# Score levels of a gated linear attention: from one head at a time to both heads in one pass, and a loop over sequences written out

## The reference, cut to what matters

```python
q = silu(x @ wq); k = sigmoid(x @ wk); v = x @ wv; f = 1 - k
g = log(f)                       # decay of each channel at each token
theta = cumsum(sign(f - 0.5)) * pi
qr = [q*cos, q*sin]; kr = [k*cos, k*sin]
# per token: S = S * exp(g) + k v^T ;  o = q S        (2 heads of 128 channels)
out = layernorm(out * sigmoid(x @ wg1 @ wg2)) @ wo
x = x + out                      # then layernorm, route to 1 of 8 experts, add
```

## Time and profile before

| | us |
|---|---|
| median of 3 runs | 716.99 |
| lowest and highest | 715.19, 717.59 |
| the profiled execution | 711.37 |
| its span, first to last instruction | 709.5 |
| routing begins | 378.98 |
| the experts' matmuls begin | 412 |

### The profile page before, as it was taken

How to read it: one execution, slowest core, us unless ns; L and a number is a source line. 1 busy time by engine, 2 the same in 40 slices (tenths; PEclk the granted TensorE clock), 3 DMA queues, 4 the chain that set the end, 5 groups by cost and what they waited for, 6 DMA issues and landing times. The chain is left out here.

```text
span 709.5 us, 13168 instructions
## 1 busy us (share of the span) xinstructions
PE 608.2 (86%) x3634; PEld 508.1 (72%) x3635; DVE 391.0 (55%) x951; ACT 281.4 (40%) x679; POOL 230.5 (32%) x344
## 2 busy tenths in 40 slices
PE   4789989869898999987463279999999999999993
PEld 2557667656666776776442179999999999999992
DVE  1486988848899898978626513323232333323231
ACT  4554667446574747654331022222222222222220
POOL 6414260511605234150302302333323233333321
PEclk9999999988999999998855579999999999999998
DMA  8900004140040302011023284554646465555410
GB/s 318 382 0 1 2 30 90 31 90 0 30 89 30 90 30 61 2 60 31 30 59 119 103 311 165 201 207 168 226 167 225 174 215 191 197 204 177 166 32 0
DMA packets 26842, 83.43 MB, mean 118 GB/s; under 512 B 3437, under 2 KB 13039, under 8 KB 20656
## 3 DMA queue, kind: packets, MB, share of 16 engines
q1 hardware_dynamic: 21120, 67.98, 28.9%
q0 software_dynamic: 4992, 14.45, 5.4%
q10 hardware_dynamic: 688, 0.52, 0.2%
HBM read 70.33 MB, written 13.52 MB: 118 GB/s over the span
## 5 line engine op out<-in xcount | busy, mean ns | idle before, releaser
L1447 DVE TENSOR_TENSOR arena<-bank_a,b_col 128x512 f32<-128x512 f32 x78 | 54.0, 692 | 190.7 <-PE bank_a L1109 177.0
L1109 PEld LDWEIGHTS bank_a<-masks,arena 128*128 128x128 f32 x1248 | 146.8, 194 | 1.9
L1109 PE MATMUL bank_a<-masks,arena 128*128 128x128 f32 x1248 | 146.9, 277 | 0.0
L1123 PE MATMUL bank_c<-w_sb,arena 128*128 x624 | 141.5, 380 | 0.9 <-ACT arena L844 0.9
L1123 PEld LDWEIGHTS bank_c<-w_sb,arena 128*128 128x128 f32 x624 | 115.5, 190 | 15.9 <-issue 1.8
L1178 DVE TENSOR_TENSOR arena<-arena 128x256 f32<-128x256 f32 x224 | 92.9, 457 | 22.1 <-PE bank_l L869 14.3
L869 PEld LDWEIGHTS bank_l<-arena,k_mix 128*128 128x128 f32 x448 | 67.1, 200 | 52.6 <-ACT k_mix L663 26.5
L869 PE MATMUL bank_l<-arena,k_mix 128*128 128x128 f32 x448 | 73.6, 290 | 18.8 <-ACT k_mix L663 11.9
L844 ACT ACTIVATE arena<-arena 128x512 f32<-128x512 f32 x78 | 45.0, 622 | 106.8 <-PE bank_c L1123 102.5
L834 ACT ACTIVATE masks<-bank_b,b_col,g_col 128x128 f32<-128x128 f32 x78 | 31.5, 453 | 132.7 <-PE bank_b L1097 132.7
L881 PE MATMUL bank_a<-arena 128*128 128x512 f32 x160 | 82.8, 616 | 0.0
(11 more groups left out here) (135 smaller groups left out, 811.0 us busy)
## 6 DMA issues: line engine op xcount, KB each, us to landing
arena<-w SPq DMA_DIRECT2D x39, 1024.0 KB
routed_rows<-arena SPq DMA_DIRECT2D x8, 1026.0 KB, 7.4
arena<-x SPq DMA_DIRECT2D x16, 512.0 KB, 3.8
w_sb<-w SPq DMA_DIRECT2D x8, 1024.0 KB, 14.2
arena<-b SPq DMA_DIRECT2D x1, 1024.0 KB, 4.3
arena<-routed_rows,take_now POOLq DMA_INDIRECT x39
out<-k_mix,put_now POOLq DMA_INDIRECT x39, 2.4
arena<-wk SPq DMA_DIRECT2D x1, 256.0 KB, 4.0
```

What stands on the lines that cost most here:

```text
L1109: m = pe.matmul(bank_a[k // 4][:, k % 4 * P:(k % 4 + 1) * P], w1_now[t.par][:, i * F + k * P:i * F + (k + 1) * P], xl_t[t.par % 2][:, i * ...
L1123: m = pe.matmul(bank_c[p][:, 0:D], h_act[:, k * P:(k + 1) * P], w2_sb[:, bass.ds(e * (FC * D) + k * D, D)], start=(k == 0), stop=(k == FC ...
L1447: dve.tensor_tensor(h_sb[:, n * 512:(n + 1) * 512].rearrange("p (k t) -> p k t", t=P), bank_a[n][:, :].rearrange("p (k t) -> p k t", t=P), ...
```

## The change

Every level function loses its head: one product loop over four pairs, one wait, updates of 512 columns, key copies of 256 columns. `need` counts semaphores per level and no longer per level and head. The pipeline loop is written out on every engine. The order on each engine is new as well: what stood between the two heads of a level now stands before or after the whole level.

```diff
@@ pipeline
-            for i in range(2):
-                at(i)
-            with eng.Fori(1, NSEQ // 2 - 1) as half:
-                for par in range(2):
-                    a = Step(half, par, 2)
-                    step(a, before(a, 1), before(a, 2), before(a, -1))
-            for i in range(NSEQ - 2, NSEQ + 2):
+            for i in range(NSEQ + 2):
                 at(i)
@@ ACT
-            def mix(b, l, h):
-                need(act, s_lev, H * LEVELS, b, H * (l - 1) + h + 1 if l > 0 else 0)
+            def mix(b, l):
+                need(act, s_lev, LEVELS, b, l)
                 for odd in range(2):
                     if l > 0:
-                        need(act, s_up, 2 * H * LEVELS, b, 2 * (H * (l - 1) + h) + odd + 1)
-                    copy(mixed_to(k_mix[l % 2], h, l, odd), mixed_from(kq[b.par], h, l, odd)).then_inc(s_mix, 1)
+                        need(act, s_up, 2 * LEVELS, b, 2 * (l - 1) + odd + 1)
+                    copy(mixed_to(k_mix[l % 2], l, odd), mixed_from(kq[b.par], l, odd)).then_inc(s_mix, 1)
                 of(a, xn_copy, 0)
-                of(b, mix, 1, 0)
                 of(a, xn_copy, 1)
-                of(b, mix, 1, 1)
+                of(b, mix, 1)
                 of(a, k_sigmoid, 0)
-                of(b, mix, 2, 0)
-                of(b, mix, 2, 1)
                 of(c, o_norm, 0)
                 of(c, o_norm, 1)
-                of(b, mix, 3, 0)
+                of(b, mix, 2)
+                of(a, k_sigmoid, 1)
                 of(c, o_norm, 2)
                 of(c, o_norm, 3)
-                of(b, mix, 3, 1)
-                of(a, k_sigmoid, 1)
+                of(b, mix, 3)
                 of(a, one_minus_k, 0)
-                of(b, mix, 4, 0)
                 of(a, q_sigmoid, 0)
                 of(c, o_copy, 0)
-                of(b, mix, 4, 1)
+                of(b, mix, 4)
+                of(a, one_minus_k, 1)
                 of(c, o_copy, 1)
-                of(a, one_minus_k, 1)
-                for l in (5, 6):
-                    for h in range(H):
-                        of(b, mix, l, h)
                 of(a, q_sigmoid, 1)
+                of(b, mix, 5)
+                of(b, mix, 6)
@@ PE
-                need(pe, s_mix, 2 * H * LEVELS, b, 2 * (H * l + h + 1))
+                need(pe, s_mix, 2 * LEVELS, b, 2 * (l + 1))
                 need(pe, s_pick, 2 * LEVELS, b, 2 * max(l - 1, 0))
-                for m in range(h * PAIRS // H, (h + 1) * PAIRS // H):
+                for m in range(PAIRS):
@@ PE step, the new order (of() left out)
+                level 0;  transposes 0, 1;  k_proj 0,0 and 0,1
+                level 1;  k_proj 1,0 and 1,1
+                level 2;  q_proj 0,0 and 0,1;  o_transposes 0
+                level 3;  o_transposes 1;  q_proj 1,0 and 1,1
+                level 4;  out_proj 0,0 and 0,1
+                level 5;  out_proj 1,0 and 1,1
+                level 6;  g1_proj 0;  k_transposes; ...
@@ DVE
-            def update(b, l, h):
-                need(dve, s_lev, H * LEVELS, b, H * l + h + 1)
+            def update(b, l):
+                need(dve, s_lev, LEVELS, b, l + 1)
                 for second in range(2):
-                    half = updated(kq[b.par], h, l, second)
-                    dve.tensor_tensor(half, half, factor(decay[b.par], h, l, second), ALU.mult).then_inc(s_up, 1)
+                    half = updated(kq[b.par], l, second)
+                    dve.tensor_tensor(half, half, factor(decay[b.par], l, second), ALU.mult).then_inc(s_up, 1)
                 def level(l):
-                    of(b, update, l, 0)
+                    of(b, update, l)
                     if l > 0:
                         of(b, pick, l - 1)
-                    of(b, update, l, 1)
```

More of the change, by code:

```diff
@@ L339, in tree, with factor @@
             return buf[:, at:at + (n >> l)]
-        def factor(buf, h, l, second):
+        def factor(buf, l, second):
             n = P >> (l + 1)
-            return strided(tree(buf, l), h * TJ * 2 * n + 1 - second, [2 * n, TJ], [2, n], [0, 2 ** l])
+            return strided(tree(buf, l), 1 - second, [2 * n, NCH], [2, n], [0, 2 ** l])
         def strided(base, at, *dims):
@@ L375, in level_queries, with updated, mixed_from, mixed_to @@
             return strided(buf, m * PAIR + Q_EVEN + h, [Q_ODD - Q_EVEN - h, 2], [2 * h, P // (2 * h)], [1, h])
-        def updated(buf, h, l, second):
+        def updated(buf, l, second):
             w = 2 ** l
-            return strided(buf, h * TJ * 2 * P + second * (P + w), [2 * P, TJ], [2 * w, P // (2 * w)], [1, w])
-        def mixed_from(buf, h, l, odd):
+            return strided(buf, second * (P + w), [2 * P, NCH], [2 * w, P // (2 * w)], [1, w])
+        def mixed_from(buf, l, odd):
             w = 2 ** l
-            return strided(buf, h * TJ * 2 * P + odd * (K_ODD + w), [PAIR, PAIRS // H], [2 * w, P // (2 * w)], [1, w])
-        def mixed_to(buf, h, l, odd):
+            return strided(buf, odd * (K_ODD + w), [PAIR, PAIRS], [2 * w, P // (2 * w)], [1, w])
+        def mixed_to(buf, l, odd):
             w = 2 ** l
-            return strided(buf, h * (PAIRS // H) * P + odd * w, [P, PAIRS // H], [2 * w, P // (2 * w)], [1, w])
+            return strided(buf, odd * w, [P, PAIRS], [2 * w, P // (2 * w)], [1, w])
         def picked(buf, l, odd):
@@ L663, in copy @@
                 return act.activation(dst, src, ACT.Copy)
-            def mix(b, l, h):
-                need(act, s_lev, H * LEVELS, b, H * (l - 1) + h + 1 if l > 0 else 0)
+            def mix(b, l):
+                need(act, s_lev, LEVELS, b, l)
                 if l == 0:
-                    need(act, s_k, H, b, h + 1)
+                    need(act, s_k, H, b, H)
                 for odd in range(2):
                     if l > 0:
-                        need(act, s_up, 2 * H * LEVELS, b, 2 * (H * (l - 1) + h) + odd + 1)
-                    copy(mixed_to(k_mix[l % 2], h, l, odd), mixed_from(kq[b.par], h, l, odd)).then_inc(s_mix, 1)
+                        need(act, s_up, 2 * LEVELS, b, 2 * (l - 1) + odd + 1)
+                    copy(mixed_to(k_mix[l % 2], l, odd), mixed_from(kq[b.par], l, odd)).then_inc(s_mix, 1)
             def normed(n, dst, src, s, j, done):
@@ L701, in one_minus_k @@
                 if h == 0:
-                    need(act, s_up, 2 * H * LEVELS, before(a, 2), 2 * H * LEVELS)
+                    need(act, s_up, 2 * LEVELS, before(a, 2), 2 * LEVELS)
                 need(act, s_k, H, a, h + 1)
@@ L814, in step @@
                 of(nxt, x_norm)
-                of(a, mix, 0, 0)
-                of(a, mix, 0, 1)
+                of(a, mix, 0)
                 of(c, zn_norm)
@@ L859, in _, with level @@
             start_at_one(pe, [s_tp, s_kz, s_qz, s_g1z, s_vz, s_gz, s_dz, s_lev, s_k7, s_kv, s_o, s_ot, s_y, s_t2, s_affz, s_zt, s_h, s_ye])
-            def level(b, l, h):
+            def level(b, l):
                 buf = kq[b.par]
@@ L928, in k_transposes @@
             def k_transposes(b):
-                need(pe, s_up, 2 * H * LEVELS, b, 2 * H * LEVELS)
+                need(pe, s_up, 2 * LEVELS, b, 2 * LEVELS)
                 need(pe, s_og, 2, b, 0)
@@ L1015, in step @@
                     pe.wait_ge(s_small, 64)
-                of(b, level, 0, 0)
+                of(b, level, 0)
                 of(a, transposes, 0)
                 of(a, transposes, 1)
-                of(b, level, 0, 1)
                 of(a, k_proj, 0, 0)
-                of(b, level, 1, 0)
                 of(a, k_proj, 0, 1)
-                of(b, level, 1, 1)
+                of(b, level, 1)
                 of(a, k_proj, 1, 0)
-                of(b, level, 2, 0)
                 of(a, k_proj, 1, 1)
-                of(b, level, 2, 1)
+                of(b, level, 2)
                 of(a, q_proj, 0, 0)
-                of(b, level, 3, 0)
                 of(a, q_proj, 0, 1)
-                of(b, level, 3, 1)
                 of(c, o_transposes, 0)
+                of(b, level, 3)
                 of(c, o_transposes, 1)
-                of(b, level, 4, 0)
                 of(a, q_proj, 1, 0)
-                of(b, level, 4, 1)
+                of(a, q_proj, 1, 1)
+                of(b, level, 4)
                 of(c, out_proj, 0, 0)
-                of(b, level, 5, 0)
                 of(c, out_proj, 0, 1)
-                of(b, level, 5, 1)
+                of(b, level, 5)
                 of(c, out_proj, 1, 0)
-                of(b, level, 6, 0)
                 of(c, out_proj, 1, 1)
-                of(b, level, 6, 1)
-                of(a, q_proj, 1, 1)
+                of(b, level, 6)
                 if b is None:
@@ L1168, in x_stats @@
                 stats("x", x_sb[a.par], a)
-            def update(b, l, h):
-                need(dve, s_lev, H * LEVELS, b, H * l + h + 1)
+            def update(b, l):
+                need(dve, s_lev, LEVELS, b, l + 1)
                 if l > 0:
                     need(dve, s_tree, LEVELS, b, l)
```

(6 more changed lines are left out.)

## The result

The changed kernel takes 764.5 us (763.7 to 768.0) where the kernel before took 717.3 beside it: ratio 1.067, 95% interval 1.063 to 1.071, 47 us slower. The forecast was 753, range 731 to 769.

What follows compares the result with a forecast made beforehand. PE's in-order list was taken to set the step pitch, DVE right behind. 32.4 + 3.2 + 5.5 + 6.0 - 11.0 = +36.1 us on the profiled 711.4 gave 747.5; 5.6 more for the median gave 753, range 731 to 769.

Steps and rivals of the forecast that it cites:

- The walk through the levels: Step 6 followed level by level: level 2 at 246.3, k_transposes 4.9 us later than before, 5.4 us a step taken.
- the ring: PE, DVE, ACT chain between score levels: bare once heads merge, PE waiting 0.6 us in most gaps, more in early ones.
- the waits on the pick: Sign of being right: PE waits 0.5 us on the pick at levels 3 to 6.
- the pitch: Time from one step's level 0 to the next: near 45 us if right, under 41 if wrong.
- rival 4: At the former jump back: straight code still makes an engine stand, +9.6 us each time, 762 us; chance 0.10.
- rival 3: In the level stretches: PE's clock falls for most of each, 3.5 us more a step, 774 us; chance 0.05.
- 1.0 a step, 6 us: Half clock on PE after the new stop before level 2, in six steps; ends 0 and 15 us.
- Steps 1 and 8: First step without c and last without a: bare ring costs 3.2 us in step 1, 5.5 in step 8.
- Written out, I let all of it go: Loop over sequences: stop at the jump 9.6 us plus register waits 1.4 us, together 11.0 us less.
- Wide instructions: DVE's updates of 512 columns save 0.8 us of DVE per step, counted as nothing because DVE does not set the pitch.
- rival 1: In the levels: ring bare, but norm before mix 2 costs little and clock holds, 2.6 us a step, 729; chance 0.14.
- rival 2: In the levels: DVE is the bound and wide instructions free it, 694 us, 700 by the median; chance 0.06.

Runs made afterwards that it cites:

- e7: Changed kernel with two extra products of 512 columns on PE before level 2, result overwritten, in the six steps with a, b and c: 759.2 us.
- e2: Changed kernel with one edit in ACT's list, o_norm 0 and 1 standing after mix 2 again: 745.3 us.
- e6: Straight code, levels one head at a time as before the change, with o_norm 0 and 1 moved before mix 2 of head 0: 725.6 us.
- e3: Changed kernel with one edit in DVE's list, each level's pick right behind its own update instead of one level late: 743.9 us.
- e4: Changed kernel with norms after mix 2, picks right behind their update, and the shift of the o norm before pick 1: 719.6 us.
- e1: Kernel before with only the loop over sequences written out, levels still one head at a time: 705.1 us.
- e5: Changed kernel with the loop over sequences put back, levels staying merged: 766.3 us.
- e9: e5 with DVE's list padded by semaphore increments, 20 ahead of the loop and 66 inside it, to the lengths of the kernel before: 776.1 us.

## Why the prediction was right

**The walk through the levels** was right. Measured from level 0 of step 6, with the predicted value in brackets: level 1 at 4.0 (4.1), level 2 at 9.4 (9.5), level 3 at 14.3 (13.3), level 4 at 17.5 (16.6), level 5 at 20.8 (19.8), level 6 at 24.1 (23.0), k_transposes at 27.2 (26.2). All but one gap fit within 0.1 us; the exception, level 2 to 3, took 4.85 instead of 3.8, and that is the low clock (e7 takes it away). Its mechanism is shown piece by piece: norms by e2 and e6, picks by e3; what remains in e4 is the ring without a second head to cover it. Two signs came out otherwise: the waits on the pick stand at levels 5 and 6 only, and the pitch is 47.7 us, not 45, in part because the old step 6 is 41.2 us and not 39.8.

**The size fell short.** The sum gave +36.1 us on the profiled execution; between the two profiled executions it is +53.9, between the medians +47.2. The 5.6 us that the prediction added to come from the profiled execution to the median do not hold for the changed kernel, whose median lies 0.7 under its profiled execution. So the forecast missed by 11.5 us where the sum behind it missed by 17.7: the 6 us between these two, and with them how well inside the range the result stands, are luck. By the number alone rival 4 (762) and rival 3 (774) lie nearer than the forecast; what speaks for the forecast is its path.

**The clock was mis-sized**, and with it the sum. "1.0 a step, 6 us" is right for the place that was meant: e7 gives 5.3 us for the fall behind level 2. But the clock falls elsewhere too. The second fall stands at the transposes of the second norm, 0.57 granted here:

```profile
253.00:257.00 4.00, 3.79 (x12) 2.95 (x13) 3.73 (x19) 2.98 (x6) 2.37 (x3) 0.57 0.01 2
```

It was there before as well, in steps 2, 3 and 6 (step 2 is the first row); the changed kernel has it in steps 3 to 7. The stretches from k_transposes to the next level 0, with it and without it, first of the kernel before (steps 6 and 5), then of the changed one (steps 6 and 2):

```profile
258.06:277.96 19.90, 18.32 (x100) 14.39 (x101) 16.06 (x43) 11.91 (x27) 11.20 (x12) 0.91 0.09 28
218.43:236.78 18.35, 16.64 (x100) 13.44 (x101) 15.12 (x41) 11.02 (x25) 11.19 (x12) 1.00 0.09 29
```

```profile
290.77:311.31 20.54, 18.44 (x101) 14.70 (x101) 16.84 (x45) 11.72 (x25) 11.89 (x14) 0.92 0.09 27
100.83:119.97 19.14, 16.90 (x100) 13.52 (x101) 15.83 (x42) 10.77 (x22) 11.88 (x14) 1.00 0.09 29
```

One such fall costs 1.4 to 1.6 us, and the change itself adds 0.6 to 0.8 to this stretch, which is the 0.67 us of the extra pick. So step 6, the one that the prediction walked through, grew by 6.6 us where 5.4 + 1.0 was forecast: it had the fall already. Steps 4, 5 and 7, which had not, grew by 7.8 to 9.0 us (step 4 counted without its stop of 9.2). All six together grew by 44 us, 7.3 a step. One step was taken as the model of six, and its own clock was not looked at. Over the whole run the time at half clock grows from some 95 to some 145 us, an estimate from the mean clocks of 0.933 and 0.905 and the two spans; how much of these 50 us was time in which PE would have waited anyway is not known.

**Steps 1 and 8** cost more than I took, for the same reason. In step 8 level 0 to k_transposes takes 27.6 us (clock 0.69) against 19.9, where I had 24.6 (the terms add up to 24.4); levels 2 to 4 run at half clock, and the gaps behind level 2, 3 and 4 are 1.0 us longer than mine. In step 1 it is 27.3 against 21.3, where I had 24.4; level 0 ran at half clock, 2.05 us, and level 1 follows after 6.2 us instead of 4.0.

**Counted as nothing** were the stretches around them: 1.0 us before level 0 of step 1, 0.7 behind its levels, 1.4 between the levels of step 8 and the third part beyond the extra pick, and 1.7 in the third part.

**The loop was credited to the wrong part.** "Written out, I let all of it go": 11.0 us; e1 shows 11.4 for the kernel before, of which 9.2 at the jump. But e5 shows that the merged levels alone take the stop away, by making DVE's list shorter (e9 brings it back with padding), and that writing the loop out then brings 1.8 us, within the uncertainty. The stop is gone in both, so the sum is the same by either way.

**Wide instructions** saved what the rows said (DVE busy 391.0 to 383.2, 7.8 us) and nothing of the time, as counted.

The rivals: rival 1 is refuted by the stop of 2.63 us; rival 2 by DVE's own idle time; rival 4 by the z_shift distances. Rival 3 is not what happened (the clock is 0.94 over the levels of step 6), yet its mechanism, the clock, supplies a large part of what is missing.

## What to carry to other kernels

Two half-size chains that take turns can hide each other's latency; merging them saves a fixed cost per instruction (0.06 us here) and lays the ring open (14.5 us here, with the best order tried). When an in-order list is rewritten, look at each instruction that now stands before a hand-over of the ring, and at what it waits for: one pair of norms cost 20 us. When one step is walked through as the model of all, read the clock of the others first: here the chosen step had a low clock that three of the others had not. A stop put down to "issue" at a loop's jump can come and go with the length of the list, so an edit that only shortens a body may seem to gain more than its work.

## What the runs showed of the hardware that I had not expected

- DVE stands 7.42 us (before) and 8.79 us (e9) at a loop's jump back, with 368 instructions in the body and 155 ahead of it by the count of the program, and not at all with 302 and 135 (e5).
- Keeping PE busy with 2.0 us of work that nobody uses (four MATMULs of 512 columns), in six steps, made the program 5.3 us faster (e7): the granted clock stayed at 1.00 instead of 0.72 in that stretch.
- Two updates of 512 columns beside POOL's tree took 1.97 to 2.25 us instead of 1.29 (changed kernel at 288.75, where the tree runs from 288.11 for 4.1 us; e4 at 255.81, tree from 255.45). The prediction had 0.8 us more for such a pair; it is 0.7 to 1.0:

```profile
288.75 1.97 DVE L1159 TENSOR_TENSOR arena<-arena 128x512 f32<-128x512 f32 x2 [0.72 <-PE bank_l L857]
```

```profile
255.81 2.25 DVE L1159 TENSOR_TENSOR arena<-arena 128x512 f32<-128x512 f32 x2 [0.44 <-PE bank_l L857]
```
